# Attention lists loaded from SyncE, counted waits on ScalarE, and batch statistics split over VectorE and ScalarE in a two-part graph network kernel

## What is computed

```python
def _gat(x, src, dst, W, a_src, a_dst, bias, n_nodes):
    H, C = a_src.shape
    xw = (x @ W).reshape(n_nodes, H, C)
    al_s = jnp.einsum('nhc,hc->nh', xw, a_src)
    al_d = jnp.einsum('nhc,hc->nh', xw, a_dst)
    logits = jax.nn.leaky_relu(al_s[src] + al_d[dst], LRELU_SLOPE)
    m = jax.lax.stop_gradient(jax.ops.segment_max(logits, dst, num_segments=n_nodes))
    e = jnp.exp(logits - m[dst])
    denom = jax.ops.segment_sum(e, dst, num_segments=n_nodes)
    alpha = e / denom[dst]
    out = jax.ops.segment_sum(alpha[:, :, None] * xw[src], dst, num_segments=n_nodes)
    return out.reshape(n_nodes, H * C) + bias

def _bn_train(x, g, b):
    mu = x.mean(axis=0)
    var = x.var(axis=0)
    return g * (x - mu) * jax.lax.rsqrt(var + BN_EPS) + b

for gw, a_s, a_d, gb, aw, ab, g, b in layers:   # widths 128->256, 256->256, 256->128, 8 heads
    res = x @ aw + ab
    x = _gat(x, src, dst, gw, a_s, a_d, gb, n) + res
    x = jax.nn.silu(_bn_train(x, g, b))
```

## Time and profile before

| | us |
|---|---|
| timed runs, median of three | 4889.73 |
| profiled execution, its own time | 4866.07 |
| its span in the trace | 4864.1 |
| GpSimd busy | 2626.7 |
| VectorE busy | 2461.6 |
| ScalarE busy | 679.2 |
| TensorE busy | 804.0 |
| gathers of the attention loops, busy | 2347.7 |
| first gather to the end of the last one, by layer | 1166.7, 1165.3, 1163.5 |
| between the loops (first to second, second to third) | 110.2, 112.8 |
| behind the third | 87.1 |

### The profile page before, as it was taken

How to read it: one execution, slowest core, us unless ns; L and a number is a source line. 1 busy time by engine, 2 the same in 40 slices (tenths; PEclk the granted TensorE clock), 3 DMA queues, 4 the chain that set the end, 5 groups by cost and what they waited for, 6 DMA issues and landing times. The chain is left out here.

```text
span 4864.1 us, 36780 instructions
## 1 busy us (share of the span) xinstructions
PE 804.0 (17%) x8458; PEld 599.6 (12%) x8458; DVE 2461.6 (51%) x3723; ACT 679.2 (14%) x2172; POOL 2626.7 (54%) x2789
## 2 busy tenths in 40 slices
PE   0667776540000000003200000000040000000002
PEld 0555544310000000003100000000030000000002
DVE  5888641335655565554455565556622333333333
ACT  2222230120000111113100010111130000010101
POOL 2000022356666666662766666666546666666663
PEclk9766788765555555556655555555565555555555
DMA  3222266423333333331333333333211211211210
GB/s 72 91 92 119 117 249 215 178 69 94 98 95 100 94 97 95 97 96 38 96 99 93 100 93 94 99 96 98 74 31 49 53 49 49 53 47 50 51 49 21
DMA packets 200298, 431.77 MB, mean 89 GB/s; under 512 B 121145, under 2 KB 123388, under 8 KB 195399
## 3 DMA queue, kind: packets, MB, share of 16 engines
q0 software_dynamic: 116080, 298.58, 22.6%
q1 hardware_dynamic: 15672, 127.31, 6.8%
q10 hardware_dynamic: 68400, 3.89, 0.9%
HBM read 371.53 MB, written 58.48 MB: 88 GB/s over the span
## 5 line engine op out<-in xcount | busy, mean ns | idle before, releaser
L499 POOL DMA_INDIRECT rows_all<-gat_tab,ell x2484 | 2347.7, 945 | 1157.1 <-issue 777.4
L1725 DVE TENSOR_TENSOR banks<-rows_all,banks 128x1848 f32<-128x1848 f32 (+3 forms) x384 | 723.6, 1884 | 1504.0 <-issue 853.2
L1729 DVE TENSOR_REDUCE acc<-banks 128x1848 f32 (+3 forms) x384 | 722.0, 1880 | 53.1
L1090 PE MATMUL banks<-ident,x_st 128*128 128x128 f32 x260 | 55.6, 298 | 3519.1 <-PEq L123 3519.1
L1090 PEld LDWEIGHTS banks<-ident,x_st 128*128 128x128 f32 x260 | 42.6, 206 | 3523.4 <-issue 3523.3
L824 ACT ACTIVATE rows_all<-acc 128x264 f32 (+1 forms) x387 | 149.8, 387 | 2028.6 <-issue 1395.5
L499 POOL DMA_INDIRECT edges<-sw_d,edge_pick x28 | 32.3, 1155 | 413.7 <-POOLq L123 401.8
L821 ACT ACTIVATE lrel<-acc 128x8 f32 x387 | 80.7, 208 | 1118.5 <-issue 992.1
L948 PE MATMUL banks<-rows_all 128*128 128x52 bf16 x4992 | 189.9, 203 | 151.2 <-PEq L123 145.8
L948 PEld LDWEIGHTS banks<-rows_all 128*128 128x128 bf16 x4992 | 179.1, 108 | 176.1 <-issue 174.4
L503 POOL DMA_INDIRECT gat_tab<-row_st,row_node x78 | 81.9, 1051 | 181.4 <-POOLq L123 83.6
(11 more groups left out here) (302 smaller groups left out, 1789.8 us busy)
## 6 DMA issues: line engine op xcount, KB each, us to landing
rows_all<-gat_tab,ell POOLq DMA_INDIRECT x2484
x_t<-adj_d SPq DMA_DIRECT2D x11, 3328.0 KB
y_t<-adj_d SPq DMA_DIRECT2D x11, 3328.0 KB
adj_d<-x_t SPq DMA_DIRECT2D x7, 3328.0 KB, 10.0
adj_d<-y_t SPq DMA_DIRECT2D x6, 3328.0 KB, 10.1
ell<-short_d ACTq DMA_DIRECT2D x204, 4.0 KB
ell<-long_d ACTq DMA_DIRECT2D x184, 4.0 KB
acc<-key_d SPq DMA_DIRECT2D x1, 1664.0 KB, 6.4
```

The lines of the kernel that those rows point to most:

```text
L499: return g.indirect_dma_start(out=dst, out_offset=None, in_=table, in_offset=bass.IndirectOffsetOnAxis(ap=idx, axis=0))
L1090: t.matmul(to, x_st[u][:, (b * kout[l] + f) * P:(b * kout[l] + f + 1) * P], ident[:, :], start=True, stop=False)
L1725: made = link.mark(v.tensor_tensor(msg_h[:, every, :, :], row_slots[u][:, every, :, :], exp_ps[:, every, :].unsqueeze(3).to_broadcast([P, ...
L1729: v.tensor_reduce(tile_of(sums, tile), by_slot, AX.X, ALU.add).then_inc(sums_made, 1)
```

## The change

Four things are done. The lists are loaded by SyncE: its own loops wait for `list_free`, which ScalarE's `copy_max` now gives, and issue the DMA; the wrapping DMA and the first four lists go there too. ScalarE no longer counts `tile_known`, `exp_in` and `sums_made` down once a chunk; it waits for u+1 and counts each down by 4 once a round, and its long and short rounds are two plain loops without the two peeled rounds. Behind the loops TensorE only transposes; VectorE adds the transposed sums to `y_t` and keeps the sums per feature. ScalarE squares each step of 256 nodes as soon as it is made, about a pivot (the first step's mean), and VectorE corrects the variance afterwards by the squared distance between mean and pivot.

```diff
@@ SyncE, at the end of its program
+            def load_list(u, lists, at):
+                sp.dma_start(ell[u][:, :], lists[:, at, :] if isinstance(at, int)
+                             else lists[:, bass.ds(at, 1), :].rearrange("p k c -> p (k c)")).then_inc(ell_landed[u], 16)
+
+            take(sp, ell_done)
...
+            sp.dma_start(long_d[:, bass.ds(long_end, 2 * RING), :], short_d[:, 0:2 * RING, :]).then_inc(ell_wrapped, 16)
+            sp.wait_ge(ell_wrapped, 16)
+            for u in range(RING):
+                load_list(u, long_d, u)
+
+            def next_lists(lists, at):
+                for u in range(RING):
+                    sp.wait_ge(list_free, u + 1)
+                    load_list(u, lists, at + u)
+                sp.sem_inc(list_free, -RING)
+
+            for l in range(3):
+                with sp.Fori(0, long_rounds_v - 1) as it:
+                    next_lists(long_d, (it + 1) * RING)
+                next_lists(short_d, short_first_v)
+                with sp.Fori(0, short_rounds_v - 1) as it:
+                    next_lists(short_d, short_first_v + (it + 1) * RING)
+                next_lists(long_d, 0)
@@ ScalarE
             def load_tile(u):
-                take(act, tile_known)
                 act.reg_load(tile_reg, ell[u][0:1, TILE_AT:TILE_AT + 1])
...
-                def one_round(size, lists, at):
+                def one_round(size):
                     for u in range(RING):
+                        act.wait_ge(tile_known, u + 1)
                         load_tile((u + 1) % RING)
-                        take(act, exp_in)
-                        copy_max()
+                        act.wait_ge(exp_in, u + 1)
+                        copy_max().then_inc(list_free, 1)
                         s.activation(weight_of[u][:, 1:size + 1, :], unit[:, 0:size, :], ACT.Copy)
                         s.activation(exp_ps[:, 0:size + 1, :], ex_in[:, 0:size + 1, :], ACT.Exp).then_inc(exp_done, 1)
-                        load_list(u, lists, at + u)
-                        take(act, sums_made)
+                        act.wait_ge(sums_made, u + 1)
                         copy_sums((u + 1) % RING).then_inc(rows_free, 1)
...
+                    for counted in (tile_known, exp_in, sums_made):
+                        act.sem_inc(counted, -RING)
+
+                for rounds, size in ((long_rounds_v, LONG), (short_rounds_v, SHORT)):
+                    with act.Fori(0, rounds):
+                        one_round(size)
                 act.sem_inc(all_summed, 1)
...
+                def square_means(step):
                     for f in range(kout[l]):
+                        at, real = (slice(step * PAIR * P, N), N - step * PAIR * P) if isinstance(step, int) else (bass.ds(step * (PAIR * P), PAIR * P), PAIR * P)
+                        act_chain(s.activation(square_ps[:, 0:real], y_t[:, f, at], ACT.Square, bias=pivot[:, f:f + 1], accum_out=bn_squares[:, f, bass.ds(step, 1)]))
+                    act_chain.reset()
+
+                take(act, means_kept)
+                act_chain(s.activation(pivot[:, 0:kout[l]], bn_parts[:, 0:kout[l], 0], ACT.Copy, scale=-1.0 / (PAIR * P)))
+                act_chain.reset()
+                with act.Fori(0, STEPS - 1) as it:
+                    square_means(it)
+                    take(act, means_kept)
+                square_means(STEPS - 1)
+                act.sem_inc(bn_done, 1)
@@ TensorE, turn_means
-                            t.matmul(to, x_st[u][:, (b * kout[l] + f) * P:(b * kout[l] + f + 1) * P], ident[:, :], start=True, stop=False)
-                            last = t.matmul(to, ident[:, :], y_t[:, f, bass.ds((step * PAIR + b) * P, P)], start=False, stop=True)
+                            last = t.matmul(to, x_st[u][:, (b * kout[l] + f) * P:(b * kout[l] + f + 1) * P], ident[:, :], start=True, stop=True)
@@ VectorE
                 def means_done(step, u):
-                    take(dve, means_kept)
+                    take(dve, xT_made)
+                    for f in range(kout[l]):
...
+                        last = v.scalar_tensor_tensor(at, made, 1.0, at, ALU.mult, ALU.add, accum_out=bn_parts[:, f, bass.ds(step, 1)])
+                    link(last)
+                    signal(means_kept)
...
-                signal(bn_in)
                 take(dve, bn_done)
-                link(v.tensor_scalar(var[:, 0:k], bn_sq[:, 0:k], 1.0 / N, BN_EPS, ALU.mult, ALU.add))
+                v.tensor_reduce(bn_sq[:, 0:k], bn_squares[:, 0:k, :], AX.X, ALU.add)
+                link(v.tensor_tensor(off_pivot[:, 0:k], mean[:, 0:k], pivot[:, 0:k], ALU.subtract))
+                v.tensor_scalar(var[:, 0:k], bn_sq[:, 0:k], 1.0 / N, BN_EPS, ALU.mult, ALU.add)
+                link(v.tensor_tensor(off_pivot[:, 0:k], off_pivot[:, 0:k], off_pivot[:, 0:k], ALU.mult))
+                link(v.tensor_tensor(var[:, 0:k], var[:, 0:k], off_pivot[:, 0:k], ALU.subtract))
```

More of the change, by code:

```diff
@@ L339, in program @@
         rows_free = sem("rows_free")
+        list_free = sem("list_free")
         pads_listed, picks_ready, pairs_gathered, lists_ready, lists_stored = (
@@ L346, in program @@
         row_made = sem("row_made")
-        means_kept, bn_in, bn_done, silu_in, silu_done = (sem(n) for n in ("means_kept", "bn_in", "bn_done", "silu_in", "silu_done"))
+        means_kept, bn_done, silu_in, silu_done = (sem(n) for n in ("means_kept", "bn_done", "silu_in", "silu_done"))
         row_ready = sem("row_ready")
@@ L837, in _ @@
                 if l == 0:
-                    take(act, ell_done)
+                    act.wait_ge(ell_wrapped, 16)
                     long_rounds_v, short_rounds_v = (act.value_load(meta[0:1, n:n + 1], min_val=2, max_val=CHUNKS // RING) for n in range(2))
[L840 to L845, removed]
                 for f in range(kout[l]):
@@ L855, in _ @@
                 if l == 0:
+                    take(act, tile_known)
                     load_tile(0)
@@ L875, in _ @@
-                with act.Fori(0, short_rounds_v - 1) as it:
-                    one_round(SHORT, short_d, short_first_v + (it + 1) * RING)
-                one_round(SHORT, long_d, 0)
+                    for counted in (tile_known, exp_in, sums_made):
[3 more added lines that the diff above has]
+                        one_round(size)
                 act.sem_inc(all_summed, 1)
-                def keep_means(step, u, turn):
-                    take(act, xT_made)
+                def square_means(step):
@@ L882, in keep_means @@
                     for f in range(kout[l]):
-                        made, col = T_ps[u][:, f * PAIR * P:(f + 1) * PAIR * P], bass.ds(step, 1)
-                        if isinstance(step, int):
-                            real = N - step * PAIR * P
-                            s.activation(y_t[:, f, N:NP], made[:, real:], ACT.Copy)
-                            last = s.activation(y_t[:, f, N - real:N], made[:, 0:real], ACT.Copy, accum_out=bn_parts[:, f, col])
-                        else:
-                            last = s.activation(y_t[:, f, bass.ds(step * (PAIR * P), PAIR * P)], made, ACT.Copy, accum_out=bn_parts[:, f, col])
@@ L890, in keep_means @@
-                    last.then_inc(means_kept, 1)
-                in_steps(act, keep_means)
-                junk_t = [af[:, f * N:(f + 1) * N] for f in range(kout[l])]
-                take(act, bn_in)
-                for f in range(kout[l]):
-                    last = s.activation(junk_t[f], y_t[:, f, 0:N], ACT.Square, bias=mean[:, f:f + 1], accum_out=bn_sq[:, f:f + 1])
-                last.then_inc(bn_done, 1)
+                        at, real = (slice(step * PAIR * P, N), N - step * PAIR * P) if isinstance(step, int) else (bass.ds(step * (PAIR * P), PAIR * P), PAIR * P)
@@ L905, in _ @@
                     last.then_inc(silu_done, high - low)
-            for n in range(1, RING):
-                act.wait_ge(ell_landed[n], 16)
         @block.tensor
```

18 lines of the change are left out of this document (11 added, 7 removed).

## The result

The changed kernel takes 4818.18 us (median of four runs, 4816.75 to 4821.39) where the one before takes 4889.11. The ratio is 0.985, with a 95% interval of 0.983 to 0.988. So it is faster by 71 us, and by 49 in the profiled executions (4816.8 against 4866.07). The forecast was 4540 us, and its range ended at 4745. The direction was right and the size was not: a fifth of the forecast gain arrived. The three loops, forecast at some 1065, 1065 and 1040 us, last 1134.5, 1146.0 and 1145.8.

The account below looks back on a forecast made before the run. GpSimd's gathers, paused by ScalarE's dragging sequencer, were taken as the bound. Gains of 323 (loops), 6 (tails), 2 (start) and 18.5 us (behind) made about 350: 4516 profiled, 4540 timed, range 4455 to 4745 us.

Parts of the forecast that it names:

- The bound of the loops: Gather loops: 828 gathers at 1.25 us would last 1035 us; 390.5 us over three loops are lost to pauses.
- The first rival: Gather loops: all pauses go, the sequencer drags no more or out of sight; 417 us gained, 4473 timed; chance 0.17.
- The drag of ScalarE's sequencer: Gather loops: while dragging, ScalarE passes one sequencer instruction every 1.37 us; the change leaves 18 a round instead of 39.
- The 26 us of loss: Short rounds, layers 0 and 1: six open instructions at the round's end (8.2 us) still lose 9 to 44 us, middle 26.
- The third: Gather loops: dragging becomes permanent, two ScalarE instructions of each chunk stand open; 473 us slower, 5363 timed; chance 0.05.
- The fourth: Gather loops: the gathers' traffic holds whatever ScalarE does; only 27 us outside the loops are won, 4863 timed; chance 0.06.
- The second: Gather loops: one ScalarE instruction of each chunk stands open, dragging 0.6 of the time; 150 us gained, 4740 timed; chance 0.15.
- The tails: Last chunks behind each loop's final gather: the same instructions go, 2 us less for each layer, 6 in all.
- Behind the loops: Work after the gather loops: 7 us gained in each of layers 0 and 1, 4.5 in layer 2; 18.5, between 5 and 25.
- The steps: Behind the loops, layers 0 and 1: half the matmuls go, a step takes 2.1 us against 2.37; 3.5 us gained.
- The squares: Behind the loops: they now lie beside the steps, so VectorE's 6.20 us wait falls to about 1.6; 3.8 us gained.
- The start: Ahead of the first gather: wrapping DMA and first lists are issued earlier, 2 us gained, between 0 and 4.5.

Follow-up runs that it names:

- the runs with fills: Kernel of its own, GpSimd alone, gathers with buffer fills before every first, third or fifth round; 420 gathers took 559 to 562 us with fills every third or fifth.
- 64-row stretch: Stretch of a kernel of its own, GpSimd gathering 64 rows instead of 128 with half the traffic: 196 gathers in 274 us, 1.40 us each.
- VectorE lighter: Changed kernel without the count instruction carrying VectorE's wait for gathered rows, 21 instead of 25 sequencer instructions a round: 4782.18 us, ratio 0.979 on the dragging chip.

## Why the prediction was wrong

**The bound of the loops.** This is the step that failed: "A loop of 828 gathers would so last 828 x 1.25 = 1035 us", and with it the 390.5 us called "lost to pauses". The 1.25 us of the earlier trace rows are what GpSimd does on an allowance of some 19 gathers. On this chip its steady rate is 1.40 us, and in no run on it did the 828 gathers take less than 1133.6 us. The kernel before came to 1166.7 / 828 = 1.409 us a gather, pauses included: it stood within 3% of the limit. That its pauses gave the allowance back, so that no gather of it was ever long, fits all of this and the runs with fills, but is a conclusion and no run of its own. Of the 131.7 us only 33 could be won, and 32 were, in layer 0. The first rival, all pauses gone, needs loops of 1035 us. They were measured only on the other chips, where the kernel before takes 4414 and 4417 us already and the change gains 14.

**The drag of ScalarE's sequencer.** Right, and better than it was put. The price is 1.40 us for each such instruction (forecast 1.37), it is passed to the round's length exactly (42.00 us for 30, 36.4 for 26), and with 18 in a round ScalarE drags nowhere. The 26 us of loss, from the six instructions that were to stand open at the round's end, did not come.

**Whose property it is.** "so this belongs to ScalarE alone" was wrong. The rule holds for VectorE, with 25 and 26 instructions in a round (35.0 and 36.4 us), and for GpSimd with its gathers. Only GpSimd's own count instructions are spared, the 17 ns of the earlier trace rows, and from these I had concluded that GpSimd was free. The trace before could have warned: a loop of 1166 us three times over, with VectorE's work cut by a third in layer 2, says that something counts gathers.

**The rivals.** None of them had this. The third was near in its thought (an engine with too many instructions holds a whole round) but named ScalarE, which has the fewest now. The fourth, that the loops would stay, came out at 4863 and is nearer to 4818 than my forecast; its reason, the traffic of the gathers, falls with the 64-row stretch. The second, at 4740, took layers 0 and 1 to gain nothing; they gained 32 and 19.

**The tails.** Forecast 2 us less for each, measured 30.7 more in all: while VectorE drags, GpSimd runs ahead of it, in layers 1 and 2 by the whole ring, and four chunks are left to do. With VectorE lighter they were 12 us shorter than before, but the stretch behind them grew by more.

**Behind the loops.** Forecast 18.5 us, measured 9.5. The steps, VectorE's timeline:

```profile
2216.81 0.69 DVE L1756 TENSOR_TENSOR x_st<-acc,den 128x512 f32 x1 [0.36 <-DVE y_t L1767]
2217.88 0.42 DVE L1767 SCALAR_TENSOR_TENSOR y_t<-banks,y_t 128x256 f32 x1 [0.38 <-DVEq L123]
...
2219.42 0.69 DVE L1756 TENSOR_TENSOR x_st<-acc,den 128x512 f32 x1 [0.77 <-DVEq L116]
...
2221.64 0.69 DVE L1756 TENSOR_TENSOR x_st<-acc,den 128x512 f32 x1 [0.36 <-DVE y_t L1767]
```

Two steps take 2221.64 - 2216.81 = 4.83 us, 2.41 each; before it was 2.37, forecast 2.1. The fused addition takes 0.42 us, less than the 0.56 taken for it. The term that was too small is the one for semaphores, 0.3: idle times of 0.38, 0.36 and 0.77 us stand between VectorE's instructions, since each waits for the last, and they come to 0.95 us in a step. That the steps gained nothing is what the Trainium skill's rule on VectorE and PSUM (Advanced Engine Details and Errata, section The Read-Write Bubble) would have given, but the time is in the waits; no run has this addition from SBUF to compare. The squares gave what was forecast: VectorE waits 1.15 and 1.67 us ahead of the variance in layers 0 and 1 where it waited 6.20.

**The start.** Forecast 2 us, measured 3.1.

## What to carry to other kernels

Before pauses are counted as time to be won, take the mean over the whole loop: if the engine's total divided by its instructions is the same in loops of different content, that mean may be near a limit, and the quick stretches may run on an allowance; the engine's work in a kernel of its own tells. Where a chip holds the engines' sequencers beside indirect gathers, count the instructions that do no arithmetic, for every engine that a round goes through, and multiply by 1.40 us: the largest product is the round, as long as the dragging lasts. A count-down for each wait, a list load from a busy queue, an instruction made only to carry a wait then cost the same as a gather, and elsewhere nothing, so measure on more than one chip.

## What was not expected of the hardware

Chips differ by 10% on the same kernel (before: 4877 and 4889 against 4414 and 4417 us), at nearly the same granted clock (0.58 and 0.59). Of the 415 us between the changed kernel's traces on two chips (4815.1 and 4400.0), 323 are in the loops and 42 in the tails; 32 lie ahead of the first of these gathers, and no run tells whether they have the same cause. Where it drags, a gather costs 1.40 us for 128 rows of 1056 or 544 bytes and for 64 rows alike, after an allowance of some 19 gathers beyond that rate; a fill ahead of every round counts like a gather (40.60 us for 28 and one). The other engines' sequencers are held at 1.40 us an instruction only while the gathers go on. What holds them is not shown by any run. Every execution here was recorded by the profiler, so none tells whether the limit is there without the recording. The Trainium skill (NOTIFIC — the notification-queue block, section Interfaces) describes a backpressure of the block that writes the engines' records, "what can stall an engine"; no run here shows whether it is at work.
